# Softmax attention: row maxima of some tiles from one pass over two key halves, with a difference made by PE and ScalarE, and PE's order taken from a scheduled list

## The reference

```python
q, k, v = (qkv[0], qkv[1], qkv[2])
scores = jnp.einsum('bhqd,bhkd->bhqk', q, k) / np.sqrt(HD).astype(np.float32)
causal = jnp.triu(jnp.ones((s, s), dtype=bool), 1)
scores = jnp.where(causal[None, None], -jnp.inf, scores)
attn_w = jax.nn.softmax(scores, axis=-1)
attn = jnp.einsum('bhqk,bhkd->bhqd', attn_w, v)
```

## Time and profile before

| | us |
|---|---|
| median of three runs | 4007.14 |
| lowest and highest | 4003.12, 4014.3 |
| the profiled execution | 4003.27 |
| its span in the trace | 4001.5 |
| core0, first score tile to last division | 271.1 to 790.3 |
| core1, the same | 1546.8 to 2283.5 |

### The profile page before, as it was taken

How to read it: one execution, slowest core, us unless ns; L and a number is a source line. 1 busy time by engine, 2 the same in 40 slices (tenths; PEclk the granted TensorE clock), 3 DMA queues, 4 the chain that set the end, 5 groups by cost and what they waited for, 6 DMA issues and landing times. The chain is left out here.

```text
span 4001.5 us, 60331 instructions
## 1 busy us (share of the span) xinstructions
PE 3295.9 (82%) x19635; PEld 2001.5 (50%) x19635; DVE 2709.7 (68%) x7212; ACT 1827.7 (46%) x2668; POOL 1012.0 (25%) x1089
## 2 busy tenths in 40 slices
PE   4559999977576967999999869789777996997898
PEld 2422333344355852222222258668656784886687
DVE  8888888576876458999999564464566455544453
ACT  1225666665122531677777725323222333553454
POOL 3442330021334631000000036427401660000000
PEclk8869999998787985999999969889877997998899
DMA  1042331000021122000000031221201112000100
GB/s 48 1 140 75 112 115 38 2 1 1 22 91 42 48 74 87 18 18 19 26 19 11 22 147 47 75 89 52 75 1 70 45 47 99 0 0 1 53 0 21
DMA packets 88138, 185.24 MB, mean 46 GB/s; under 512 B 24560, under 2 KB 43056, under 8 KB 84784
## 3 DMA queue, kind: packets, MB, share of 16 engines
q1 hardware_dynamic: 60704, 116.03, 8.7%
q0 software_dynamic: 26576, 64.79, 5.4%
q10 hardware_dynamic: 576, 0.79, 0.1%
HBM read 119.92 MB, written 60.82 MB: 45 GB/s over the span
## 5 line engine op out<-in xcount | busy, mean ns | idle before, releaser
L2127 ACT ACTIVATE core_pr<-core_two 128x1024 f32<-128x1024 f32 (+3 forms) x896 | 794.4, 933 | 442.2 <-PE core_two L2089 441.3
L2153 DVE TENSOR_REDUCE core_mx<-core_one 128x1 f32<-128x512 f32 x1280 | 800.9, 682 | 23.1 <-PE core_one L2073 19.6
L2073 PE MATMUL core_one<-arena,core_q_sb 64*128 64x512 bf16 (+3 forms) x1792 | 548.4, 380 | 107.1 <-DMA core_q_sb<-core_q_sb 44.7
L2073 PEld LDWEIGHTS core_one<-arena,core_q_sb 64*128 64x128 bf16 x1792 | 140.6, 94 | 690.7 <-DVE core_mx L2153 525.8
L2100 PE MATMUL core_ps_o<-core_pr,core_vals 128*32 128x512 f32 (+3 forms) x3584 | 438.9, 562 | 1.6 <-ACT core_oT L2131 0.5
L2089 PE MATMUL core_two<-core_q_sb,arena 64*128 64x512 bf16 (+3 forms) x1792 | 362.5, 362 | 6.4 <-ACT core_pr L2127 5.4
L2150 DVE CUSTOM_DVE_ANT_0 core_junk<-core_one,behind 128x128 bf16<-128x128 f32 (+3 forms) x512 | 230.3, 486 | 58.4 <-PE core_one L2073 53.0
L2021 POOL COPY core_vals<-arena 128x288 f32<-128x288 f32 x32 | 14.5, 455 | 982.6 <-PE core_ps_o L2100 982.5
L341 POOL DMA_INDIRECT expert_out<-arena,moe_first_dest_index x142 | 139.6, 983 | 98.1 <-ACT arena L514 84.7
L341 POOL DMA_INDIRECT expert_out<-arena,moe_second_dest_index x142 | 139.9, 985 | 96.8 <-ACT arena L514 82.8
L451 PE MATMUL moe_second_bank<-arena 128*128 x1136 | 152.0, 277 | 5.7 <-ACT arena L514 5.3
(11 more groups left out here) (538 smaller groups left out, 7431.1 us busy)
## 6 DMA issues: line engine op xcount, KB each, us to landing
arena<-expert_out SPq DMA_DIRECT2D x64, 256.0 KB, 3.0
core_q_sb<-q_parts SPq DMA_DIRECT2D x384, 32.0 KB
arena<-k_parts SPq DMA_DIRECT2D x360, 32.0 KB
expert_rows<-arena SPq DMA_DIRECT2D x16, 512.0 KB, 11.8
core_w_raw<-in_m_up POOLq DMA_DIRECT2D x25, 256.0 KB, 4.3
m_hi<-core_w_hi POOLq DMA_DIRECT2D x25, 256.0 KB, 2.8
m_lo<-core_w_lo POOLq DMA_DIRECT2D x25, 256.0 KB, 3.4
q_parts<-qkv_parts SPq DMA_DIRECT2D x16, 384.0 KB, 2.6
```

Of the source, the lines that this page charges most:

```text
L2073: pe.matmul(one[bank][:, 0:width], q_sb[rows, hq, pair, qt * P:(qt + 1) * P], k_sb[rows, hq, pair, kc * CW:kc * CW + width], start=True, s ...
L2127: a.activation(pr[:, k % 2, hp, :, off:CW], two[hp][:, :, off:CW], ACT.Exp, scale=HD ** -0.5).then_inc(s_exp, 1)
L2153: v.tensor_reduce(mx[:, h * TPB + qt, kc:kc + 1], one[bank][:, 0:width], AX.X, ALU.max).then_inc(s_read, 1)
```

## The change

A unit is a pair of heads and a query tile (16 in a group). Some units are folded: the keys are taken as two halves of equal width, a and b. PE forms the scores of half a in a bank of `one`, as before, and the difference b - a of both heads in a wide buffer of `two`: scores with half b, and on top of them scores with the keys of half a negated (`k_neg`, made by POOL once a group). ACT takes the relu of the difference into `over` (SBUF, float32, two buffers). DVE then adds a + relu(b - a) and takes its maximum in one `tensor_tensor_reduce`, so that one pass over half the keys replaces the passes over all. In core0 the mask goes into the difference by a matmul.

Which units: in core1 every third (5 of 16), in core0 those of query tiles 5 and 7 (4 of 16); in group 0 all but the first two (and in core0 but those of query tile 0), in group 1 the same for its first six units and the usual ones behind. That makes 842 first-pass tiles in core1 (1024 before) with 91 differences, and 630 in core0 (768 before) with 76. A steady group has 54 and 40 tiles.

`order()` replaces `plan`, `banked` and `over_groups`: it walks through the stage once, with a cost for each operation written in the code, and picks at each point one of the possible next operations of PE. The list is then issued as it stands. By it, the first second of core0 follows 50 first-pass tiles (32 of group 0, 18 of group 1), and that of core1 52 (36 and 16). Within a pair of matmuls the side used last goes second or first as `turns` says. `mx` is doubled. Loads, waits and counters are rewritten with it: the wide buffers share one counter. Memsets are written as 4-byte words, the two small copies in `q_sb` fall away for the first four groups, and ACT's queue issues the key loads of groups 0 and 1. In the diff, empty lines and unchanged parts are left out.

```diff
+TWO_ONES = float(np.uint32(0x3F803F80).view(np.float32))
...
+    N = BATCH * GROUPS
+    q_sb = st.sb("q_sb", [P, GROUPS, PAIRED, SEQ], BF16)
+    k_neg = st.sb("k_neg", [P, 2, PAIRED, CW], BF16)
     junk = st.sb("junk", [P, 3, CW], BF16)
+    over = st.sb("over", [P, 2, 2, CW])
...
+    mx = st.sb("mx", [P, 2, GH * TPB, 2])
...
+    NOTE, PIPE, REACH, WEIGH_LEAD = 60, 170, 12, -300
+    def folded(n, u):
+        pair, qt = units[u]
+        if n == 0 or n == 1 and u < 6:
+            return 2 <= u and (qt > 0 or not causal)
+        return qt in (5, 7) if causal else u % 3 == 2
+    def half(qt):
+        return (qt + 1) * P // 2 if causal else CW
+    def tiles(n, u):
+        qt = units[u][1]
+        if folded(n, u):
+            return [(side, half(qt), 0) for side in range(2)]
+        keys = (qt + 1) * P if causal else SEQ
+        return [(side, min(CW, keys - kc * CW), kc) for kc in range(-(-keys // CW)) for side in range(2)]
+    def order():
+        firsts = {n: [("first", n, u, i) for u in range(len(units)) for i in range(len(tiles(n, u)))] for n in range(N)}
+        todo = []
+        for n in range(N):
+            late = firsts[n + 1][:4] if n + 1 < N else []
+            early = firsts[n][4:] if n else firsts[n]
+            todo += [*early, ("rows", n, 0, 0), *late[:2], ("turn", n, 0, 0), *late[2:], ("split", n, 0, 0)]
+        plain = [e for e in todo if e[0] == "first" and folded(e[1], e[2]) and e[3] == 0]
...
+        while weigh < N * N2 or first < len(todo) or moves or norms:
+            options = []
+            while first < len(todo) and todo[first][0] in ("rows", "split"):
+                e = todo[first]
+                n = e[1]
+                events.append(e)
+                if e[0] == "rows":
+                    done[e] = dve(0, 250)
+                else:
+                    done["turn", n, 0, 0] = dve(done["turned", n], 1250) - 500 + NOTE
+                    done["known", n] = at["dve"] + 5000
+                first += 1
+            if first < len(todo):
+                e = todo[first]
+                n, u = e[1:3]
+                if e[0] == "turn":
+                    options.append((max(ring_free(), done["rows", n, 0, 0] + NOTE), at["dve"], "turn", e))
+                elif n <= second // (2 * N2) + 2:
+                    if not folded(n, u) or ("diff", n, u, 0) in done:
+                        options.append((ring_free(), at["dve"], "first", e))
+            if diff < len(plain) and plain[diff][1] <= second // (2 * N2) + 2 and todo.index(plain[diff]) - first < REACH:
+                e = plain[diff]
+                near = todo.index(e) - first
+                if diff < 2 or ("read", plain[diff - 2][1], plain[diff - 2][2]) in done:
+                    options.append((wide_free(), at["act"] - (3000 if near < 3 else 0), "diff", ("diff", e[1], e[2], 0)))
+            if second < 2 * N * N2:
...
+            _, n, k, i = e
+            events.append(e)
+            if what == "first":
+                width = tiles(n, k)[i][1]
+                ring.append(e)
+                seen = issue(ready, width * 5 // 24 + 30) + NOTE
+                if folded(n, k):
+                    seen = max(seen, done["diff", n, k, 0])
...
+            elif what == "diff":
+                w = half(units[k][1])
+                wide.append(e)
+                seen = issue(ready, w * 5 // 6 + (107 if causal else 0) + 60) + NOTE
+                if diff >= 2:
+                    seen = max(seen, done["read", plain[diff - 2][1], plain[diff - 2][2]])
+                done[e] = act(seen, w * 5 // 3 + 100) + NOTE
+                diff += 1
...
-    def over_groups(eng, emit):
-        whole, head, tail = range(N1), range(HEAD), range(HEAD, N1)
-        def group(b, hq, firsts, before, second=True, more=1):
-            for what, k, ahead, bank in banked(plan(firsts, second, more), before):
-                emit(what, k, *after(b, hq, ahead), bank)
-        group(0, 0, [(0, whole), (1, head)], [], False, 0)
...
+    events = order()
...
+    def fetch_rows(eng, side, n):
+        b, hq = divmod(n, GROUPS)
+        dst, src = ((q_sb, q_parts), (k_sb, k_parts))[side]
+        for r, pair in enumerate(PAIRS):
+            rows = src[pair[side], hq * GH * HD:(hq + 1) * GH * HD, b * SEQ:(b + 1) * SEQ].rearrange("(h y d) t -> y d h t", y=2, d=HD)
+            for y in range(2):
+                at = y * HALF + r * HD
+                eng.dma_start(dst[at:at + HD, hq], rows[y]).then_inc(s_loaded[hq], 16)
...
+            def load(n):
+                hq = n % GROUPS
+                if n >= GROUPS:
+                    sp.wait_ge(s_filled, spot["second", n - GROUPS, N2 - 1, 1] + 1)
+                else:
                     sp.wait_ge(s_zero, hq + 1)
                     sp.wait_ge(s_ones, hq + 1)
-                for side, (dst, src) in enumerate(((q_sb, q_parts), (k_sb, k_parts))):
...
+                fetch_rows(sp, 0, n)
+                if n >= 2:
+                    fetch_rows(sp, 1, n)
+                if n >= GROUPS:
+                    for y in range(2):
+                        at = y * HALF + QK_ROWS
+                        sp.dma_start(q_sb[at:at + 3, hq], q_sb[at + 3:at + 6, hq]).then_inc(s_loaded[hq], 16)
...
+                p.memset(q_sb[:, hq].bitcast(F32), 0.0).then_inc(s_zero, 1)
...
+            def turn_sign(n):
+                hq = n % GROUPS
+                p.wait_ge(s_loaded[hq], fetched(n))
+                if n >= 2:
+                    p.wait_ge(s_filled, last_diff[n - 2] + 1)
+                p.tensor_scalar(k_neg[:, n % 2], k_sb[:, hq, :, 0:CW], -1.0, None, ALU.mult).then_inc(s_knegs, 1)
...
+                b, hq = divmod(n, GROUPS)
+                if n >= 2:
+                    p.wait_ge(s_weighed, (n - 1) * N2)
                 p.tensor_copy(vals[:, hq % 2, :, :, 0:HD + 1],
-                              values[:, bass.ds(b * TPB, TPB), hq * GH:(hq + 1) * GH, :]).then_inc(s_vals, 1)
+                              values[:, b * TPB:(b + 1) * TPB, hq * GH:(hq + 1) * GH, :]).then_inc(s_vals, 1)
...
+            turn_sign(0)
...
+            def turns(side, later):
+                if side is not None:
+                    return 1 - side, side
+                begin = tiles(*later[1:3])[later[3]][0] if later and later[0] == "first" else 0
+                return begin, 1 - begin
...
+                elif what == "diff":
+                    pair, qt = units[k]
+                    w, into = half(qt), two[spot[e] % 2]
+                    if spot[e] == first_diff[n]:
+                        pe.wait_ge(s_knegs, n + 1)
+                    if spot[e] >= 2:
+                        pe.wait_ge(s_wide, spot[e] - 1)
+                    if causal:
+                        for side in range(2):
+                            pe.matmul(into[:, side, w - P:w], g.mask_k, g.identb[:], start=True, stop=False, skip_group_check=True)
+                    both = turns(None if causal else last, later)
+                    for side in both:
+                        rows, _ = lane(side)
+                        pe.matmul(into[:, side, 0:w], q_sb[rows, hq, pair, qt * P:(qt + 1) * P], k_sb[rows, hq, pair, w:2 * w],
+                                  start=not causal, stop=False, skip_group_check=True)
+                    for side in both:
+                        rows, _ = lane(side)
+                        mm = pe.matmul(into[:, side, 0:w], q_sb[rows, hq, pair, qt * P:(qt + 1) * P], k_neg[rows, n % 2, pair, 0:w],
+                                       start=False, stop=True, skip_group_check=True)
+                    mm.then_inc(s_filled, 1)
+                    last = both[1]
...
+                elif what == "second":
                     c, j, off, mask = steps[k]
-                    hp = int(what[-1])
-                    if k == 0 and hp == 0:
+                    into = two[spot[e] % 2]
+                    if k == 0 and i == 0:
                         pe.wait_ge(s_mld, (n + 1) * 32)
-                    pe.wait_ge(s_exp, (n * N2 + k) * 2 + hp + 1)
+                    if spot[e] >= 2:
+                        pe.wait_ge(s_wide, spot[e] - 1)
                     if mask:
-                        for i in range(2):
-                            pe.matmul(two[hp][:, i, off:off + P], g.identb[:], g.mask_k, start=True, stop=False, skip_group_check=True)
-                    for i in range(2):
-                        rows, pair = lane(hp * 2 + i)
-                        mm = pe.matmul(two[hp][:, i, off:CW], k_sb[rows, hq, pair, j * P:(j + 1) * P],
+                        for side in range(2):
+                            pe.matmul(into[:, side, off:off + P], g.identb[:], g.mask_k, start=True, stop=False, skip_group_check=True)
+                    both = turns(None if mask else last, later)
...
+            for n in range(2):
+                a.wait_ge(s_ones, n + 1)
+                fetch_rows(a, 1, n)
+            for e in events:
...
+                elif what == "diff":
```

(49 more changed lines are left out.)

353 lines of the change are left out of this document (179 added, 174 removed).

## The result

The changed kernel took 3918.95 us (median of 4 runs, 3914.25 to 3925.48), the kernel before 4007.11 on the same chip: a ratio of .9779, 95% interval .9759 to .98. That is 88 us less where I had forecast 117; 3919 lies inside the range. The profiled execution took 3914.25 us.

The account below looks back on a forecast made before the run. VectorE was taken to bound core1, with PE near its limit in core0. Core1 pace 60 and head 24, core0 pace 22 and head 10 made 116 us less: 3887, stated as 3890, range 3838 to 3955.

Parts of the forecast that it names:

- rivals D: Whole kernel: relu and exponential need different tables, two loads of 1.28 us per difference, total 4320; chance 2%.
- E: Whole kernel: the fold buys nothing in the paces and the starts cost the head gain, total 4007; chance 3%.
- Core1's pace, 39.1 forecast: Full attention stage, steady groups: 43.2 us a group falls to 39.1, saving 60 us over 14.6 groups.
- the base of 36: Core1 steady group: three engines within 10% at 36 to 37 us; VectorE 35.9, ScalarE 35.7, PE 34.2 to 39.9.
- The factor of 92%: Core1 pace: 36 us at 92%, chosen between a lone bound's 97% and VectorE's 86% in core0, giving 39.1.
- Rival A: Both paces: balanced engines lock more than expected, core1 41.5, core0 30.5 us a group, total 3947; chance 25%.
- Rival B: Both paces: the list packs nearly perfectly, core1 37.2, core0 27.6 us a group, total 3843; chance 15%.
- Core0's pace, 28.9 forecast: Causal attention stage, steady groups: 30.5 us falls to 28.9, PE's sum with about half the first tiles paired; 22 us saved.
- Heads, 27 and 34 forecast: Stage starts before the first exponential: core0 37.35 to 27 us, gain 10; core1 58.9 to 34 us, gain 24.
- The 0 that I took for it: Smaller edits at stage starts: k_neg's cost against earlier starts nets 0 for both stages together, ends -4 and +5 us.
- priced in the pace: Order list: the greedy list replaces even spacing, takes no instruction away, and gets no gain beyond the forecast paces.
- Rival C: Attention stages: relus hold up exponentials and VectorE starves; slower once each difference costs .7 us, 4057 at 1 us; chance 5%.

Follow-up runs that it names:

- the quota: Planner rule added to the changed kernel's list, keeping second products near an even share of first tiles: 1.0131 of the kernel before without differences, .994 with differences and guards.
- a better list: Changed kernel with first k_neg on VectorE, plus planner durations, preferences and a small quota set per stage, other units folded: 3982.61 us, .9676 of the kernel before.
- Its control: Changed kernel, differences kept, with the quota and two guards added to its list: .994 of the kernel before, core1 pace 40.08, core0 34.7.
- the kernel with other costs: Changed kernel with traced durations in the list's planner (mask pair .30 for .107, weighing .23 above its columns for .14) and two guards: .9961 of the kernel before.

## Why the prediction was right or wrong

- **Bound and direction.** Right. VectorE held core1 before; taking 6 us a group from it and giving 4 to ScalarE let the pace fall until PE bound. Relu prices, tile counts (842 and 630) and the absence of table loads beside the relus came as said; rivals D and E are out. With the relu on ScalarE the trace gives 40.10 in core1. The Trainium skill, page "ScalarE: Activation LUTs", section "Rules for kernel authors", puts relu on VectorE and gives as its reason VectorE's speed in bf16; by that rule, as worked out ahead, the pace would have stayed at 43.2. No run tried that.
- **Core1's pace, 39.1 forecast, 40.10 measured (14 of the 29 us missed).** The step that failed is the base of 36. I had PE's sum as 34.2 to 39.9 and then took the 36 of VectorE and ScalarE as if PE's were no higher. PE's own sum is 37.2, the middle of my bounds (37.05), where half of the first tiles pair up: just what I took in core0 and did not take here. The factor of 92% for engines that wait for each other was good: 37.17 / 40.10 is 93%. But it was a choice between two busy shares and not worked out from waits, so that it came so close is in part luck. Rival A's mechanism is real but 2.9 us large and inside my factor; its 41.5 was not reached. Rival B's 37.2 is PE's own sum, the pace without any wait.
- **Core0's pace, 28.9 forecast, 29.69 measured (10 us missed).** The PE sum with half of the first tiles paired came out close: 28.7 measured. But I took the sum as the pace and left out the waits, 1.0 us, though I had counted them in core1.
- **Heads, 27 and 34 forecast, 29.8 and 36.7 measured (4 us of the gain missed).** `k_neg` took 2.78 us, outside my bounds of 1.2 to 2.5, and PE stood behind it once a stage. The 0 that I took for it together with the earlier start did not hold: core0's first tile starts when it did before (271.03 against 271.06), and outside the stages only 3 us went in all. With it on VectorE the heads are 27.2 and 34.1, as forecast. Both head sums had PE at 1.2 GHz throughout, though, and the granted clock was .73 and .75 (.81 and .80 with `k_neg` on VectorE); in core0, where I let PE set the head, the close number is in part luck.
- **The list, "priced in the pace".** Half wrong. Without differences the new list, with the edits that belong to it, costs 2.5 us a group in core1 and 1.1 in core0 (with the quota) or 2.8 and 5.8 (without). With the differences the quota makes no odds in core1, but a better list is worth another 1.6. The trip of the maxima, which I had called covered, is covered in this kernel; the runs without differences show the price where it is not.
- **Rival C** (lockstep): no wait before a relu is over 1.2 us, and their 25.2 us over 55 relus of core1's steady part are .46 each, under my turning point of .7; and the kernel is faster, not slower.

What stays open: how core0's gain of .8 us a group splits between differences and list. Its control failed on `k_neg`, and no other run has the changed kernel's list there without them.

## What to carry to other kernels

When work is moved off the engine that binds, the new pace is the largest sum of the others plus waits: work out every engine's own sum and put the factor for waits on the largest, not on the one you were looking at. A list that a greedy planner makes is tuned to the balance it was made for: take away part of the work and the kernel may get slower than it was before the change, so "undo half" is no neutral experiment. When two idle engines could do the first instruction that PE's queue waits for, give it to the faster one.

## What the runs showed of the hardware

- A multiplication by -1 of 1024 bf16 elements a partition took 2.78 us on POOL and .43 on VectorE, 6.5 times less, though POOL's cast of 512 elements takes .61.
- Short stalls of PE were followed by a stretch at 1.2 GHz (.50 granted) in two kernels: after 3.36 us idle the clock was .50 from 581 to 584 (the kernel with other costs), and after a window with 1.50 busy us of 4 it was .50 from 2161 to 2169 (the list without differences). The heads ran at .73 and .75, with 162 and 130 matmuls in 29.8 and 36.7 us, where the kernel before had .50 with 74 and 98 in 37.4 and 58.9.
- Three engines that share three narrow and two wide buffers of PSUM were busy 98.5, 99.5 and 93% (VectorE, ScalarE, PE) at a pace of 35.28 when the weighings were cut to bf16. With PE's own sum at 37.2, about 2 us above that pace, they ran at 40.10, 7% over the largest sum.
